# Row numbers of the first tile loaded apart, gathers without a memset between them, and finer waits in the top layers, in a recommendation tower's forward pass

## The chip, the cores and the metric

The kernel runs on one core of one Trainium2 chip. The metric is the device time of one execution in microseconds; the median of three executions before the change is 874.92 us (874.81 to 875.81).

## The reference, cut to what matters

```python
# ids (2048, 32); tbl_f (v_f, 64) with v_f 1000 to 125000; kernels (496, 64, 64); all f32
e = jnp.stack([tbl_f[ids[:, f]] for f in range(32)], axis=1)          # (2048, 32, 64)
II, JJ = np.triu_indices(32, k=1)                                     # 496 pairs
z = jnp.sum(e, axis=-1)                                               # (2048, 32)
outer = jnp.einsum('bpd,pde,bpe->bp', e[:, II], kernels, e[:, JJ])    # (2048, 496)
h = jnp.concatenate([z, outer, dense_ctx], axis=1)                    # (2048, 544)
h = jnp.maximum(h @ W_top1 + b_top1, 0.0)                             # 512 wide
h = jnp.maximum(h @ W_top2 + b_top2, 0.0)                             # 256 wide
y = h @ W_top3                                                        # (2048, 1)
```

For each sample 32 table rows are gathered, all 496 pairs of rows are multiplied through a 64 x 64 matrix of their own, and the results go through three small layers.

## The kernel before, in words

**Tiles.** The batch of 2048 is cut into six tiles of 128, 128, 256, 512, 512 and 512 samples. A "couple" k is the two tables 2k and 2k + 1; a tile has 16 couples. For each table and each 128 samples GpSimd issues one indirect DMA (L369), 512 in all, into one of eight slots of `rows`; an indirect DMA reads its row numbers from `ids_sb`, which SyncE loads whole in one transfer (L379) ahead of everything else. In the first tile GpSimd also executes a memset of a spare buffer before each gather (L368) and waits for the memset before (L367). A gather of couple n >= 8 waits until the couple eight before it has been transposed and summed.

**Steps.** When both tables of a couple have landed, TensorE transposes them (L598, `transpose_couples`) and ScalarE copies the result into `xt` (L414). VectorE sums each row for z (L535). A step (`do_step`, L615) multiplies two 64-row halves of `xt` by two 64 x 128 blocks of the pair kernels `kw`, into a PSUM bank `y`; the two halves use the upper and the lower 64 rows of the array. VectorE multiplies the result with the partner's rows (L563), and TensorE sums over the products with a strip of ones (L632, `sum_group`), into an accumulator that ScalarE copies into `h_in` (L445). The 128 steps of a tile fill four chunks of `h_in`. In narrow tiles several steps share a bank (`pack`: 4, 4, 2, 1, 1, 1). There are three `y` banks, taken in turn by all of TensorE's uses. Field sums and dense inputs are transposed (L644) into `z_in`.

**Top layers.** `mlp1` (L662, L667) is done in two pairs of 128 outputs, each with four chunks of `h_in` (128 rows) and a 64-row part of `z_in`; `mlp2` (L678) has four chunks of `h1` and two outputs halves; `mlp3` (L688) two chunks of `h2`. ScalarE applies bias and Relu (L469, L482), two activations each, and counts `act_read` up once behind the second. TensorE waits for that count (L654, L673, L684). The tables in the trace count each f32 matmul as two records.

**Order.** `PLAN` is one list by hand that all engines walk. The top layers of tile t - 1 stand in tile t, behind the first group of steps and then 8, 16 and 24 steps later (`MLP_STEPS`), each block followed by more steps; the last group of sums of tile t - 1 comes directly before the first block. For the last tile all four blocks follow its last sums at the end of the kernel. Couples 0 to 7 of the first tile are placed directly before the first step that needs them. SyncE's queue holds, in order: the row numbers, 17 chunks of `kw` (8.4 MB), biases and `w3`, `w1`, `w1z`, `w2`, and the dense inputs of each tile (L399).

Of the kernel before, what the change touches and what calls it, by code (L numbers as in the profile page):

```python
# [4 lines left out]
P = 128  # L5
# [11 lines left out]
Y_SLOTS = 3  # L17
# [110 lines left out]
PAIR_STEPS = [8, 20, 36, 56, 72, 84, 100, 116]  # L128
PAUSED_TILES = 1
MLP_STEPS = (0, 8, 16, 24)  # L130
# [77 lines left out]
def copy_use(t, k):  # L208

    for what in (("couple", t, k), ("couples", t, k), ("couples", t, k - 1)):  # L210
        if what in Y_USES:
            return Y_USES[what]
# [42 lines left out]
def tower_program(nc, dense, ids, tables, pair_k, w1, w1z, b1, w2, b2, w3, out):  # L255
# [4 lines left out]
    with ExitStack() as ctx:  # L260
# [25 lines left out]
        ident = sb("ident", [P, P])  # L286
        spare = sb("spare", [P, 2 * P])
        ones_strip = sb("ones_strip", [P, 62])

        y_banks = [bank(f"y{i}", [P, 2, TILE]) for i in range(Y_SLOTS)]  # L290
        accs = [bank(f"acc{i}", [P, TILE]) for i in range(2)]

        ids_loaded = sem("ids_loaded")
        ident_zeroed = sem("ident_zeroed")
# [7 lines left out]
        y_read = sem("y_read")  # L302
        act_read = sem("act_read")
        summed = sem("summed")
        acc_read = sem("acc_read")
        paused = sem("paused")
        fields_summed = sem("fields_summed")
# [30 lines left out]
        def _(pool):  # L338
# [5 lines left out]

            pool.wait_ge(ids_loaded, 16)
            for t in range(TILES):
                for k in range(COUPLES):
                    n = couple(t, k)
# [6 lines left out]
                    for h in range(2):  # L355
                        for c in range(rowsets(t)):
# [3 lines left out]
                            if steps > 0:  # L360

                                pool.wait_ge(y_read, steps)
                            elif t < PAUSED_TILES:
                                pauses = 2 * rowsets(t) * k + rowsets(t) * h + c
                                if pauses > 0:

                                    pool.wait_ge(paused, pauses)  # L367
                                pool.memset(spare[:], 0.0).then_inc(paused, 1)  # L368
                            pool.indirect_dma_start(  # L369
# [8 lines left out]
        def _(sp):  # L378
            sp.dma_start(ids_sb[:], ids).then_inc(ids_loaded, 16)  # L379
            first = 0  # L380
# [22 lines left out]
        def _(act):  # L403
# [50 lines left out]
            def read_mlp1(t, pair):  # L454
                u = y_use("mlp1", t, pair)
                w = WIDTHS[t]
                if t == 0 and pair == 0:

                    act.wait_ge(small_loaded, 48)
                elif pair == 0:  # L460

                    act.wait_ge(y_full, y_use("mlp2", t - 1, 0) + 1)

                    act.wait_ge(out_stored, 16 * t)

                act.wait_ge(y_full, u + 1)
                for h in range(2):
                    j = 2 * pair + h
                    last = nc.scalar.activation(h1[:, j, 0:w], y_banks[u % Y_SLOTS][:, h, 0:w], ACT.Relu,  # L469
                                                bias=b1_sb[:, j:j + 1])  # L470
                last.then_inc(act_read, 1)

            def read_mlp2(t):
# [6 lines left out]
                act.wait_ge(y_full, u + 1)  # L480
                for j in range(J2):
                    last = nc.scalar.activation(h2[:, j, 0:w], y_banks[u % Y_SLOTS][:, j, 0:w], ACT.Relu,  # L482
                                                bias=b2_sb[:, j:j + 1])
                last.then_inc(act_read, 1)

# [32 lines left out]
        def _(dve):  # L518
# [47 lines left out]
            for what, t, n in PLAN:  # L566
                if what == "couple":
                    field_sums(t, n)
                elif what == "couples":
                    field_sums(t, n)  # L570
                    field_sums(t, n + 1)
                elif what == "step" and n in runs[t]:
# [3 lines left out]
        def _(pe):  # L576
# [71 lines left out]
            def mlp1(t, pair):  # L648
                if pair == 0:
# [3 lines left out]

                    pe.wait_ge(acc_read, CHUNKS * (t + 1))  # L654

                    pe.wait_ge(act_read, act_uses_through(y_use("fields", t, 0)))
                w = WIDTHS[t]
                y = take_y(y_use("mlp1", t, pair))
                for h in range(2):
                    j = 2 * pair + h  # L660
                    for c in range(CHUNKS):
                        nc.tensor.matmul(y[:, h, 0:w], w1_sb[:, c, j * P:(j + 1) * P], h_in[:, c, 0:w],  # L662
                                         start=c == 0, stop=False)
                for h in range(2):
                    part = slice(DIM * h, DIM * h + DIM)
                    j = 2 * pair + h
                    last = nc.tensor.matmul(y[:, h, 0:w], w1z_sb[part, j * P:(j + 1) * P], z_in[part, 0:w],  # L667
                                            start=False, stop=True)
                last.then_inc(y_full, 1)

            def mlp2(t):

                pe.wait_ge(act_read, act_uses_through(y_use("mlp1", t, 1)))  # L673
                y = take_y(y_use("mlp2", t, 0))
                w = WIDTHS[t]
                for j in range(J2):
                    for c in range(J1):
                        last = nc.tensor.matmul(y[:, j, 0:w], w2_sb[:, c, j * P:(j + 1) * P], h1[:, c, 0:w],  # L678
# [3 lines left out]
            def mlp3(t):  # L682

                pe.wait_ge(act_read, act_uses_through(y_use("mlp2", t, 0)))  # L684
                y = take_y(y_use("mlp3", t, 0))
                w = WIDTHS[t]
                for c in range(J2):
                    last = nc.tensor.matmul(y[0:1, 0, 0:w], w3_sb[:, c:c + 1], h2[:, c, 0:w],  # L688
                                            start=c == 0, stop=c == J2 - 1)
# [76 lines left out]
```

## Time and profile before

| | |
|---|---|
| median of three executions | 874.92 us |
| profiled execution | 875.68 us |
| its span, first to last instruction | 873.9 us |
| TensorE (PE) busy | 840.1 us, 96% |
| VectorE (DVE) busy | 623.2 us, 71% |
| GpSimd (POOL) busy | 494.5 us, 57% |
| ScalarE (ACT) busy | 151.9 us, 17% |
| DMA | 28.32 MB |

The profiled execution is one execution; what its span leaves out (1.8 us) lies before the first and behind the last instruction. In the timelines PE is matmul and PEld the weight load; a letter q behind an engine is its queue or sequencer. "idle before" is the engine's time without work before an instruction, with what released it. A chain of waits is followed back from the last instruction: at each step to what released it.

### The profile page before, as it was taken

The page shows a single profiled execution, that of the slowest core. Times are in us where ns is not written, and L with a number is a line of the kernel's source. Part 1 is how long each engine was busy: PE and PEld are TensorE (multiplying, and loading weights), DVE is VectorE, ACT ScalarE, POOL GpSimd, SP SyncE. Part 2 cuts the span into 40 slices and gives each one's busy share as a digit, 9 for nine tenths or more (in the row PEclk, how much of TensorE's full clock was granted, in tenths as well). Part 3 has the DMA queues.
Part 4 walks back from the last instruction along what each step waited for, and adds up shares of the span by engine and source line. Part 5 has one row for each costly group of instructions (what it writes and reads, how often), then busy time and mean ns, then how long its engine had stood idle before and what let it go on. Part 6 is the DMA issues. An engine that isn't in the chain of part 4 may idle for free.

```text
span 873.9 us, 15786 instructions
## 1 busy us (share of the span) xinstructions
PE 840.1 (96%) x6584; PEld 404.9 (46%) x6584; DVE 623.2 (71%) x706; ACT 151.9 (17%) x273; POOL 494.5 (57%) x550
## 2 busy tenths in 40 slices
PE   1899999999999999999999999999999999999997
PEld 1788888766655333333333333333333333333332
DVE  0677577688866788888855488888845588888840
ACT  1212312212210220020210320020211312020001
POOL 7875777777777777777776477667723430000000
DMA  9511111111111111111111011111100000000000
GB/s 325 187 28 23 28 31 29 28 28 31 28 28 27 28 27 27 30 28 27 28 26 25 17 25 26 23 27 27 26 12 13 16 14 1 1 1 1 1 1 1
DMA packets 24209, 28.32 MB, mean 32 GB/s; under 512 B 13254, under 2 KB 13385, under 8 KB 24012
## 3 DMA queue, kind: packets, MB, share of 16 engines
q0 software_dynamic: 16384, 16.81, 10.7%
q1 hardware_dynamic: 7744, 10.49, 3.6%
q8 instruction: 54, 0.88, 0.4%
q14 instruction: 15, 0.12, 0.0%
q10 hardware_dynamic: 12, 0.01, 0.0%
HBM read 27.27 MB, written 0.01 MB: 31 GB/s over the span
## 4 chain that ended last, share of the span: by engine, by line
PE 92%; DVE 3%; POOL 2%; DMA 1%; issue 1%; ACT 1%; DVEq 0%; ACTq 0%
PE y L615 50%; PE acc L632 26%; PE y L662 7%; PE y L598 4%; PE y L678 3%; DVE prod L563 3%; POOL rows L369 2%; PE y L667 1%; DMA rows<-tbl,ids_sb 1%; PE y L688 1%; POOL spare L368 1%; DMA ids_sb<-ids 0%; ACT h_in L445 0%; PE y L644 0%; ACT h L482 0%
## 5 line engine op out<-in xcount | busy, mean ns | idle before, releaser
L563 DVE TENSOR_TENSOR prod<-y,xt 128x1024 f32<-128x1024 f32 (+2 forms) x600 | 582.4, 1033 | 199.4 <-PE y L615 198.3
L369 POOL DMA_INDIRECT rows<-tbl,ids_sb x512 | 483.4, 944 | 214.0 <-issue 111.2
L615 PE MATMUL y<-xt,kw 64*128 64x512 f32 (+2 forms) x2976 | 476.9, 463 | 4.3 <-DVE prod L563 3.2
L615 PEld LDWEIGHTS y<-xt,kw 64*128 64x128 f32 x2976 | 244.0, 190 | 217.0 <-issue 199.4
L632 PE MATMUL acc<-prod,ones_strip 128*32 128x512 f32 (+2 forms) x2976 | 239.4, 454 | 0.3 <-DVE prod L563 0.3
L632 PEld LDWEIGHTS acc<-prod,ones_strip 128*32 128x32 f32 x2976 | 79.4, 109 | 142.4 <-issue 68.1
L414 ACT COPY xt<-y 128x1024 f32<-128x1024 f32 (+3 forms) x56 | 36.2, 646 | 300.8 <-PE y L598 300.7
L662 PE MATMUL y<-h_in,w_sb 128*128 128x512 f32 (+2 forms) x192 | 58.4, 457 | 3.1 <-ACT h_in L445 2.6
L598 PE MATMUL y<-ident,rows 128*128 128x128 f32 x256 | 41.4, 289 | 20.5 <-DMA rows<-tbl,ids_sb 20.4
L535 DVE TENSOR_REDUCE z_rows<-rows 128x8 f32<-128x512 f32 (+2 forms) x96 | 44.6, 500 | 17.2 <-DMA rows<-tbl,ids_sb 17.2
L445 ACT COPY h_in<-acc 128x512 f32<-128x512 f32 (+2 forms) x24 | 10.6, 443 | 240.4 <-PE acc L632 240.4
L598 PEld LDWEIGHTS y<-ident,rows 128*128 128x128 f32 x256 | 28.0, 142 | 45.5 <-issue 33.3
L662 PEld LDWEIGHTS y<-h_in,w_sb 128*128 128x128 f32 x192 | 31.1, 190 | 31.2 <-issue 21.5
L678 PE MATMUL y<-h,w_sb 128*128 128x512 f32 (+2 forms) x96 | 28.9, 454 | 1.4 <-ACT h L469 1.4
L469 ACT ACTIVATE h<-y,b_sb 128x512 f32<-128x512 f32 (+2 forms) x24 | 11.8, 541 | 83.0 <-PE y L667 83.0
L678 PEld LDWEIGHTS y<-h,w_sb 128*128 128x128 f32 x96 | 15.6, 191 | 13.2 <-issue 10.6
L433 ACT COPY xt<-xt 64x1024 f32<-64x1024 f32 (+2 forms) x24 | 18.3, 762 | 0.6
L431 ACT COPY xt<-xt 64x1024 f32<-64x1024 f32 (+2 forms) x24 | 18.2, 758 | 0.6
L429 ACT COPY xt<-xt 64x512 f32<-64x512 f32 (+2 forms) x24 | 11.4, 474 | 15.6 <-DVE prod L563 15.4
L368 POOL MEMSET spare<- 128x256 f32 x32 | 10.5, 327 | 2.0 <-DMA ids_sb<-ids 2.0
L430 ACT COPY xt<-xt 64x512 f32<-64x512 f32 (+2 forms) x24 | 11.4, 476 | 0.6
L435 ACT COPY xt<-xt 64x512 f32<-64x512 f32 (+2 forms) x24 | 11.4, 475 | 0.6
(22 smaller groups left out, 55.1 us busy)
## 6 DMA issues: line engine op xcount, KB each, us to landing
rows<-tbl,ids_sb POOLq DMA_INDIRECT x512
kw<-pair_k SPq DMA_DIRECT2D x14, 512.0 KB, 11.9
w_sb<-w SPq DMA_DIRECT2D x1, 1024.0 KB, 12.2
w_sb<-w SPq DMA_DIRECT2D x1, 512.0 KB, 13.6
kw<-pair_k SPq DMA_DIRECT2D x1, 384.0 KB, 18.3
ids_sb<-ids SPq DMA_DIRECT2D x1, 256.0 KB, 2.7
kw<-pair_k SPq DMA_DIRECT2D x1, 256.0 KB, 4.2
w1z_sb<-w1z SPq DMA_DIRECT2D x1, 256.0 KB, 12.3
```

Of the source, the lines that this page charges most:

```text
L368: pool.memset(spare[:], 0.0).then_inc(paused, 1)
L369: pool.indirect_dma_start(out=rows[:, s, c, h, :], out_offset=None, in_=tables[f], in_offset=bass.IndirectOffsetOnAxis(ap=ids_sb[:, b, f:f ...
L414: nc.scalar.copy(xt[:, s:s + count, 0:w], y_banks[u % Y_SLOTS][:, 0:count, 0:w]).then_inc(act_read, 1)
L431: nc.scalar.copy(xt[DIM:P, x0:x3 + 1:3, 0:w], xt[DIM:P, d:d + 1, 0:w].to_broadcast([DIM, 2, w])).then_inc(extra_made, 1)
L433: nc.scalar.copy(xt[0:DIM, x1:x2 + 1, 0:w], xt[0:DIM, e:e + 1, 0:w].to_broadcast([DIM, 2, w])).then_inc(extra_made, 1)
L535: nc.vector.reduce_sum(z_rows[:, 0:rowsets(t), 0, 2 * k:2 * k + 2], rows[:, n % GATHER_SLOTS, 0:rowsets(t), :, :], axis=mybir.AxisListType ...
L563: nc.vector.tensor_tensor(prod_part(t, d, n), y_part(t, d, n), x, ALU.mult).then_inc(y_read, n)
L598: last = nc.tensor.transpose(y[:, h, P * c:P * c + P], rows[:, s, c, :, :].rearrange("p h d -> p (h d)"), ident[:])
L615: last = nc.tensor.matmul(y[:, h, :], kw[part, d, :], xt[part, slot_of(t, units[h][0] // 2), 0:w], start=True, stop=True)
L632: last = nc.tensor.matmul(acc[32 * q:32 * q + 32, 0:w], ones_strip[:, 30 - 2 * s:62 - 2 * s], prod_part(t, u // 2)[:, u % 2, :], start=s = ...
L662: nc.tensor.matmul(y[:, h, 0:w], w1_sb[:, c, j * P:(j + 1) * P], h_in[:, c, 0:w], start=c == 0, stop=False)
L678: last = nc.tensor.matmul(y[:, j, 0:w], w2_sb[:, c, j * P:(j + 1) * P], h1[:, c, 0:w], start=c == 0, stop=c == J1 - 1)
```

## The change

The row numbers come in two transfers, first those of the first tile (16 KB), then the rest (240 KB), each with a semaphore; GpSimd waits for the second at the second tile. The memset and its wait between the first tile's gathers are gone, with the spare buffer. Each Relu activation counts up a semaphore: the first of two `half_read`, the second `act_read`. `mlp1` now waits at first for three chunks of `h_in`, multiplies these and the field part for both halves, and then waits for the fourth and multiplies it for both. `mlp2` loops over chunks outside and output halves inside, and waits for each chunk; `mlp3` waits for each half of `h2`. Two rewritings in `copy_use` and the VectorE loop change no instruction.

```diff
-PAUSED_TILES = 1
...
+        first_ids_loaded = sem("first_ids_loaded")
...
+        half_read = sem("half_read")
...
-            pool.wait_ge(ids_loaded, 16)
+            pool.wait_ge(first_ids_loaded, 16)
             for t in range(TILES):
+                if t == 1:
+
+                    pool.wait_ge(ids_loaded, 16)
...
-                            elif t < PAUSED_TILES:
-                                pauses = 2 * rowsets(t) * k + rowsets(t) * h + c
-                                if pauses > 0:
-
-                                    pool.wait_ge(paused, pauses)
-                                pool.memset(spare[:], 0.0).then_inc(paused, 1)
...
-            sp.dma_start(ids_sb[:], ids).then_inc(ids_loaded, 16)
+            sp.dma_start(ids_sb[:, 0:rowsets(0), :], ids[:, 0:rowsets(0), :]).then_inc(first_ids_loaded, 16)
+            sp.dma_start(ids_sb[:, rowsets(0):, :], ids[:, rowsets(0):, :]).then_inc(ids_loaded, 16)
...
-                for h in range(2):
+                for h, done in enumerate((half_read, act_read)):
                     j = 2 * pair + h
-                    last = nc.scalar.activation(h1[:, j, 0:w], y_banks[u % Y_SLOTS][:, h, 0:w], ACT.Relu,
-                                                bias=b1_sb[:, j:j + 1])
-                last.then_inc(act_read, 1)
+                    nc.scalar.activation(h1[:, j, 0:w], y_banks[u % Y_SLOTS][:, h, 0:w], ACT.Relu,
+                                         bias=b1_sb[:, j:j + 1]).then_inc(done, 1)
...
-                for j in range(J2):
-                    last = nc.scalar.activation(h2[:, j, 0:w], y_banks[u % Y_SLOTS][:, j, 0:w], ACT.Relu,
-                                                bias=b2_sb[:, j:j + 1])
-                last.then_inc(act_read, 1)
+                for j, done in enumerate((half_read, act_read)):
+                    nc.scalar.activation(h2[:, j, 0:w], y_banks[u % Y_SLOTS][:, j, 0:w], ACT.Relu,
+                                         bias=b2_sb[:, j:j + 1]).then_inc(done, 1)
...
-                    pe.wait_ge(acc_read, CHUNKS * (t + 1))
-
                     pe.wait_ge(act_read, act_uses_through(y_use("fields", t, 0)))
+
+                    pe.wait_ge(acc_read, CHUNKS * (t + 1) - 1)
...
-                    for c in range(CHUNKS):
+                    for c in range(CHUNKS - 1):
                         nc.tensor.matmul(y[:, h, 0:w], w1_sb[:, c, j * P:(j + 1) * P], h_in[:, c, 0:w],
                                          start=c == 0, stop=False)
...
-                    last = nc.tensor.matmul(y[:, h, 0:w], w1z_sb[part, j * P:(j + 1) * P], z_in[part, 0:w],
-                                            start=False, stop=True)
+                    nc.tensor.matmul(y[:, h, 0:w], w1z_sb[part, j * P:(j + 1) * P], z_in[part, 0:w],
+                                     start=False, stop=False)
+
+                pe.wait_ge(acc_read, CHUNKS * (t + 1))
+                for h in range(2):
+                    j = 2 * pair + h
+                    last = nc.tensor.matmul(y[:, h, 0:w], w1_sb[:, CHUNKS - 1, j * P:(j + 1) * P],
+                                            h_in[:, CHUNKS - 1, 0:w], start=False, stop=True)
                 last.then_inc(y_full, 1)
 
             def mlp2(t):
-
-                pe.wait_ge(act_read, act_uses_through(y_use("mlp1", t, 1)))
-                y = take_y(y_use("mlp2", t, 0))
+                u = y_use("mlp2", t, 0)
                 w = WIDTHS[t]
-                for j in range(J2):
-                    for c in range(J1):
+                for c in range(J1):
+                    if c % 2 == 0:
+
+                        pe.wait_ge(half_read, 3 * t + c // 2 + 1)
+                    else:
+
+                        pe.wait_ge(act_read, act_uses_through(y_use("mlp1", t, c // 2)))
+                    if c == 0:
+                        y = take_y(u)
+                    for j in range(J2):
                         last = nc.tensor.matmul(y[:, j, 0:w], w2_sb[:, c, j * P:(j + 1) * P], h1[:, c, 0:w],
                                                 start=c == 0, stop=c == J1 - 1)
                 last.then_inc(y_full, 1)
 
             def mlp3(t):
 
-                pe.wait_ge(act_read, act_uses_through(y_use("mlp2", t, 0)))
+                pe.wait_ge(half_read, 3 * t + 3)
                 y = take_y(y_use("mlp3", t, 0))
                 w = WIDTHS[t]
                 for c in range(J2):
+                    if c == J2 - 1:
+
+                        pe.wait_ge(act_read, act_uses_through(y_use("mlp2", t, 0)))
```

## Rows read from the trace of the kernel before

**Rows 1.** page, part 1: engine, busy us (share of the span), instructions

```profile
PE 840.1 (96%) x6584; PEld 404.9 (46%) x6584; DVE 623.2 (71%) x706; ACT 151.9 (17%) x273; POOL 494.5 (57%) x550
```

**Rows 2.** waits of TensorE, whole span: us in total, times, longest us

```profile
PE y L598 <- DMA rows<-tbl,ids_sb: 20.4, 7, 11.9
...
PE y L662 <- ACT h_in L445: 2.6, 4, 0.7
PE y L688 <- ACT h L482: 1.4, 1, 1.4
PE y L678 <- ACT h L469: 1.4, 1, 1.4
...
PE y L662 <- issue: 0.4, 1, 0.4
```

**Rows 3.** timeline of PE, first tile: start us, us, line, shapes, count [idle before]

```profile
11.87 0.45 PE L598 MATMUL y<-ident,rows 128*128 128x128 f32 x1 [11.87 <-DMA rows<-tbl,ids_sb]
...
22.75 0.47 PE L598 MATMUL y<-ident,rows 128*128 128x128 f32 x1 [0.56 <-DMA rows<-tbl,ids_sb]
...
25.98 2.08 PE L615 MATMUL y<-xt,kw 64*128 64x128 f32 x16
28.88 0.47 PE L598 MATMUL y<-ident,rows 128*128 128x128 f32 x1 [0.82 <-DMA rows<-tbl,ids_sb]
29.29 3.79 PE L615 MATMUL y<-xt,kw 64*128 64x128 f32 x32
...
36.17 1.16 PE L615 MATMUL y<-xt,kw 64*128 64x128 f32 x16 [0.16 <-DVE prod L563]
```

**Rows 4.** chain that ended last, three pieces: start us, us, what

```profile
0.75 2.65 DMA ids_sb<-ids
...
22.82 6.02 DMA rows<-tbl,ids_sb
...
233.63 2.37 DMA rows<-tbl,ids_sb
```

**Rows 5.** busy time by stretch: engines' busy us, granted clock, DMA share, GB/s

```profile
12.00:30.00 18.00, 9.83 (x61) 7.18 (x63) 5.55 (x15) 3.85 (x13) 15.87 (x26) 1.00 1.03 386
```

**Rows 6.** timeline of SP and POOL, start of the first tile

```profile
0.75 0.38 SPq L379 DMA_DIRECT2D ids_sb<-ids  x1
...
3.92 1.10 POOL L369 DMA_INDIRECT rows<-tbl,ids_sb  x1 [0.16 <-issue]
...
5.52 0.95 POOL L369 DMA_INDIRECT rows<-tbl,ids_sb  x1 [0.17 <-issue]
...
6.96 0.95 POOL L369 DMA_INDIRECT rows<-tbl,ids_sb  x1 [0.17 <-issue]
```

**Rows 7.** timeline of POOL, start of the second tile

```profile
51.27 0.94 POOL L369 DMA_INDIRECT rows<-tbl,ids_sb  x1 [0.30 <-issue]
```

**Rows 8.** page, part 6: DMA issues, count, KB each, us to landing

```profile
kw<-pair_k SPq DMA_DIRECT2D x1, 128.0 KB, 2.5
```

**Rows 9.** chain that ended last, around two first-layer blocks in mid-kernel

```profile
90.13 0.92 PE y L615 x16
...
456.17 3.63 PE y L615 x16
...
461.65 7.06 PE y L662 x16
468.72 1.06 PE y L667 x4
469.78 3.44 PE y L615 x16
```

**Rows 10.** timeline of the weight loads (PEld) of L662

```profile
844.59 0.19 PEld L662 LDWEIGHTS y<-h_in,w_sb 128*128 128x128 f32 x1 [0.24 <-issue]
```

**Rows 11.** timeline of the tail, ACT and PE

```profile
859.99 1.26 ACT L469 ACTIVATE h<-y,b_sb 128x512 f32<-128x512 f32 x2 [6.78 <-PE y L667]
...
869.86 1.88 PE L688 MATMUL y<-h,w_sb 128*1 128x512 f32 x4 [1.42 <-ACT h L482]
```

More of the change, by code:

```diff
@@ L208, in copy_use @@
 def copy_use(t, k):
-    for what in (("couple", t, k), ("couples", t, k), ("couples", t, k - 1)):
+    for what in [("couple", t, k)] + [("couples", t, k), ("couples", t, k - 1)]:
         if what in Y_USES:
@@ L286, in tower_program @@
         ident = sb("ident", [P, P])
-        spare = sb("spare", [P, 2 * P])
         ones_strip = sb("ones_strip", [P, 62])
@@ L303, in tower_program @@
         act_read = sem("act_read")
+        half_read = sem("half_read")
         summed = sem("summed")
         acc_read = sem("acc_read")
-        paused = sem("paused")
         fields_summed = sem("fields_summed")
@@ L569, in _ @@
                 elif what == "couples":
-                    field_sums(t, n)
-                    field_sums(t, n + 1)
+                    for k in range(n, n + 2):
+                        field_sums(t, k)
                 elif what == "step" and n in runs[t]:
```

## The prediction, made before the changed kernel was run

> **What bounds the kernel now.** I began with the page's first part: TensorE is busy for 840.1 us, 96% of the span [rows 1]. So a microsecond counts only where TensorE stands still, or where its instructions get longer. The view of who waited for whom, kept to TensorE, gives all of its stops [rows 2]: 20.4 us for gathered rows, 2.6 + 0.4 us in front of the first top layer (L662), and 1.4 us each in front of the second (L678) and the third (L688). The change aims at exactly these; everything else in the 873.9 us stays.
>
> Where the 20.4 us lie the timeline tells. The seventh couple of tables (k = 6) is the last that TensorE waits for in the first tile: it is idle for 0.82 us and transposes at 28.88, and from there on the steps carry it [rows 3]. The chain of waits says who is late: one gather's data, 6.02 us from the start of its issue to landing [rows 4]. In this stretch the DMA engines are full: their share is 1.03 from 12 to 30 us, at 386 GB/s, most of it the pair kernels `kw` [rows 5]. A gather in a quiet stretch takes 2.37 us by the same view [rows 4].
>
> **Part 1, head of the kernel.** GpSimd issues the first tile's 32 gathers with a memset before each: 5.52 to 6.96 is 1.44 us per gather [rows 6]. In the second tile, where no memset stands between, one takes 0.94 us after 0.30 us of issue, 1.25 us start to start [rows 7]. So 0.19 us goes for each gather behind the first.
> The row numbers landed at 0.75 + 2.65 = 3.40 us [rows 4], and the first gather started at 3.92 [rows 6]. Without the memset it needs some 0.3 us of issue [rows 7], so 0.2 us is won. The transfer shrinks from 256 KB to 16 KB. No row has this size; the nearest is 128 KB of `kw` in 2.5 us [rows 8] against 2.65 for the 256 KB [rows 4]. That would give 0.15 us, and the same slope carried on to 16 KB 0.3; I take 0.2. The ends are 0 (all is latency) and 0.6 us. The second transfer of row numbers puts one more issue on SyncE ahead of all of `kw`, 0.38 us by the first one's row [rows 6]. Nothing feels that: a chunk of `kw` of 128 KB lands after 2.5 us [rows 8], and TensorE has no rows to work on before 11.87 [rows 3]. The new wait at the second tile is for a transfer that has been in for 40 us by then.
> Couple 6 ends with the 14th gather: 0.2 + 0.2 + 13 x 0.19 = 2.9 us earlier. If the time to landing stays at 6.02 us, its rows are there at 28.84 - 2.9 = 25.9. Can TensorE take them? Couple 4 (10th gather) comes 2.1 us earlier, at 20.6 instead of 22.75. From there to the end of couple 5's steps TensorE needs at today's rates 28.06 - 22.75 = 5.3 us [rows 3], which ends at 25.9. So both arrive together and all 2.9 us are won, with next to no slack. What is late next: couple 7 was wanted at 33.0, after the 3.79 us of couple 6's steps, and comes by the same count by 28.4, wanted then at 30.1; couple 8 comes by 31.0 and is wanted behind one more group, at about 30.1 + 1.6 = 31.7 (an estimate between 16 records' 1.16 and 2.08 us). The second of these covers by 0.7 us only. Later gathers have the eight slots as their bound, not the pace.
> Ends for this part: 0, if landings do not follow the issue, and 4.6 us, if TensorE's rate changes too (rival 2).
>
> **Part 2, the first top layer in tiles 0 to 4.** The wait for the fourth chunk now stands behind three chunks and the field sums. At 512 wide a full block of 16 matmul records takes 7.06 us [rows 9], so twelve take 5.3, far more than the copy of the last chunk. The stops in front of L662 (3.0 us, [rows 2]) go: four put down to the copy, with the longest at 0.7 us, which I take to be the tail's, and one of 0.4. That leaves 2.3 us in mid-kernel.
> But the order of kinds changes. After a full-height block the steps' 16 records of 64 rows take 3.63 us, directly after the field matmuls (64 rows as well) 3.44 [rows 9]: 0.19 us for the change from full height to half. The four field records show it too: 1.06 us, where a quarter of 3.44 is 0.86. The other direction is seen in the full block: the weight loads come every 0.19 + 0.24 = 0.43 us [rows 10], 16 x 0.43 = 6.88, and it takes 7.06: again 0.18. At 128 wide the steps behind the field matmuls take 0.92 us in the chain [rows 9], against 1.16 behind a stop [rows 3], so a narrow tile pays as well. Today the order is sum, full, field, step: two changes of height per pair. It becomes sum, full, field, full, step: four. Ten pairs of the five tiles lie between steps, where TensorE has no slack: 10 x 2 x 0.19 = 3.8 us lost. Ends: 1.9 (if only the change to half height costs) and 4.0. So the middle loses 3.8 - 2.3 = 1.5 us.
> The Trainium skill (TensorEngine Tiling (Array Packing), the numbered limits of tiling) says that changing the tiling mode drains the engine. It gives no time; the trace agrees, with 0.19 us.
>
> **Part 3, the tail.** Behind the last step nothing covers anything. In front of L662: 0.7 us go. In front of L678: 1.4 us go, for chunks 0 and 1 come from the pair read long before; their four matmuls take 4 x 0.88 = 3.5 us, and the first of the two activations [rows 11] ends after 0.63. In front of L688: two activations, 1.26 us as in the layer before, become one, 0.63 [rows 11]; the second is hidden behind the first matmul, half of 1.88 us. 0.6 us go. Changes of height: sum, full, field, full, field, full both before and after (the new last block of pair 0 runs on into pair 1), so no loss. Tail: 2.7 us. The mlp2 order (chunks outside, halves inside) changes no count and no shape; the new increments ride on activations. I cost them at nothing.
>
> **Sum.** 2.9 (head) - 1.5 (middle) + 2.7 (tail) = 4.1 us. The profiled execution took 875.68 us, 0.8 over the median, with a span of 873.9; it would become 871.6 and the span 869.8. Against the median of 874.92 the forecast is 870.8 us. A measurement here can tell about 0.2% (1.75 us) from no change.
>
> **Rivals.**
> Rival 1: the landings do not follow. With the engines at a share of 1.03 a gather is served between the large packets of `kw`; if the queue's share of them sets the pace, earlier issues only wait longer. For it: 6.02 against 2.37 us to landing [rows 4]. Against: a queue that falls behind would show a growing time to landing, and it does not grow: the second gather, issued from 5.52 [rows 6], lets TensorE start at 11.87 [rows 3], 6.35 us later, the fourteenth after 6.02. The head gives 0 and the time is 873.7: no change by the bound.
> The Trainium skill (DMA: Bandwidth & Descriptors, section on SWDGE, HWDGE and iDMA) says that the engine goes round-robin between the queues of the two kinds; by that a gather waits its turn but is not crowded out, and the sum would be mine.
> Rival 2: TensorE's rate rises sooner. The granted clock stands at 1.00 (2.4 GHz) from 12 to 30 us [rows 5], but the step records say otherwise: 16 of them take 2.08 us at 25.98 and 1.16 at 36.17, and the 32 at 29.29 still 3.79 [rows 3]: the rate of the lower level, 1.2 GHz, up to 33.0. In front of that rise TensorE had stopped twice for gathers (0.56, 0.82). With gathers earlier those stops shrink and work comes closer together; if couple 6's 32 records run fast, 3.79 becomes some 2.1: 1.7 us more, 869.1.
> Rival 3: the rise stays at 33.0 whatever TensorE does. Then the work between 30.1 and 33.0 is at the slow rate, two groups at 0.92 us extra each: the head gives 1.1 and the time is 872.6.
> Rival 4, slower than before: the denser but thinner stream puts the rise off further. From 30.1 us on, slow work costs 0.79 of its fast time (2.08 / 1.16). To end over 876.7 it must eat 4.1 + 1.8 = 5.9 us: 7.5 us of fast work, done in 13.4, so the low rate would last to 43.5 us instead of 33. It decides from there on. Against: TensorE has fewer stops than before; for: the column does not show the level, so I can't see what moves it.
> The skill (TensorE: Matmul & The Clock Gate, the part on the clock gate) warns that trn2's clock events in a trace can be unreliable; rows 3 against rows 5 bear it out.
>
> **How the numbers follow.** Forecast 0.47; rival 1 0.15; rival 2 0.15; rival 3 0.17; rival 4 0.06. Rivals 1 and 3 give the slow side, rival 3 straddles the 0.2% bound (873.2) with a quarter of its chance. Faster 0.47 + 0.15 + 0.13 = 0.75, same 0.15 + 0.04 = 0.19, slower 0.06. Range: rival 2 with the large end of the row numbers' transfer and 0.5 us for small errors, 868.4; above rival 1 with 0.2 us, 873.9. Rival 4 and what spills over the ends is left out.
>
> **What would show it.** Gathers start every 1.25 us from 3.5; couple 6's transpose is at 26.0 and the first fast steps 3 us earlier. No stop in front of L662 and L678, 0.6 to 0.8 left in front of L688. In the middle every first-layer pair is 0.38 us longer, split by the field matmuls. The time from the end of the last sum to the end is 2.7 us shorter. I am wrong in the head if the transpose of couple 6 is later than 27, in the middle if blocks of four full matmuls behind the fields run without a gap, in the tail if a stop over 0.2 us is left in front of L678.

## The result, and the profile after

Four executions of each kernel, alternating on one chip: 868.95 us median after (868.28 to 869.07) against 875.37 before. The ratio is 0.9925, 95% interval 0.9908 to 0.9942, so 6.4 us are gone where 4.1 were forecast; 868.95 lies inside the range of 868.4 to 873.9, near its lower end. The profiled span went from 873.9 to 867.2 us, by 6.7, and it is this pair of executions that is taken apart below. One execution of each can carry up to 1.3 us that are not the change's: of 23 executions of the kernel before, in the experiments' first group, nine took 874.05 to 874.62 us and fourteen 875.35 to 876.47, and the one taken apart here, at 875.68, belongs with the upper ones. What parts the two is not shown, since the one trace of this kernel is of the upper kind.

The page of the changed kernel, parts 1 and 2 in part:

```profile
span 867.2 us, 15755 instructions
PE 842.1 (97%) x6584; PEld 403.7 (47%) x6584; DVE 622.6 (72%) x706; ACT 151.9 (18%) x273; POOL 483.9 (56%) x518
```

TensorE is busy for 2.0 us more than before [rows 1], in a span 6.7 us shorter. So 8.7 us of its stops went, and 2.0 of that were paid back in work. Its waits, by the same view as [rows 2]:

```profile
PE y L593 <- DMA rows<-tbl,ids_sb: 16.1, 4, 10.9
PE y L610 <- DVE prod L558: 3.5, 9, 0.7
PE y L698 <- ACT h L478: 0.8, 1, 0.8
```

The wait for gathered rows fell from 20.4 us in seven places to 16.1 in four. The waits of the first and second top layer (now L657 and L685) are gone from the list, and the third (L698) keeps 0.8 of 1.4.

To see where the time went I put marks into both timelines and compared their times. The kernel before, TensorE, at its first group of sums, at the gather wait that follows 230 us, and at its last group of sums:

```profile
37.27 1.95 PE L632 MATMUL acc<-prod,ones_strip 128*32 128x128 f32 x64
...
236.05 0.65 PE L598 MATMUL y<-ident,rows 128*128 128x128 f32 x4 [0.71 <-DMA rows<-tbl,ids_sb]
...
841.00 1.92 PE L632 MATMUL acc<-prod,ones_strip 128*32 128x512 f32 x16 [0.29 <-DVE prod L563]
```

The changed kernel at the same three places:

```profile
33.04 1.96 PE L627 MATMUL acc<-prod,ones_strip 128*32 128x128 f32 x64
...
231.67 1.09 PE L593 MATMUL y<-ident,rows 128*128 128x128 f32 x8
...
837.13 1.92 PE L627 MATMUL acc<-prod,ones_strip 128*32 128x512 f32 x16 [0.29 <-DVE prod L558]
```

The head is 4.2 us shorter (37.27 to 33.04), at the last sums the lead (how much earlier the changed kernel is at the same place) is 3.9 (841.00 to 837.13), at the end 6.7. So the **head gives 4.2** (forecast 2.9), the **middle costs 0.4** (forecast 1.5) and the **tail gives 2.8** (forecast 2.7). The eight transposes at 231.67 run through, where four of them waited 0.71 us before.

The head of the changed kernel, GpSimd and TensorE:

```profile
2.68 1.10 POOL L365 DMA_INDIRECT rows<-tbl,ids_sb  x1 [1.21 <-DMA ids_sb<-ids]
4.08 0.94 POOL L365 DMA_INDIRECT rows<-tbl,ids_sb  x1 [0.30 <-issue]
5.33 0.94 POOL L365 DMA_INDIRECT rows<-tbl,ids_sb  x1 [0.30 <-issue]
```

```profile
17.51 0.48 PE L593 MATMUL y<-ident,rows 128*128 128x128 f32 x1 [2.00 <-DMA rows<-tbl,ids_sb]
17.92 2.08 PE L610 MATMUL y<-xt,kw 64*128 64x128 f32 x16
...
25.18 0.47 PE L593 MATMUL y<-ident,rows 128*128 128x128 f32 x1
25.58 2.94 PE L610 MATMUL y<-xt,kw 64*128 64x128 f32 x32
28.45 0.33 PE L593 MATMUL y<-ident,rows 128*128 128x128 f32 x1
29.25 1.16 PE L610 MATMUL y<-xt,kw 64*128 64x128 f32 x16 [0.47 <-DVE prod L558]
```

The gathers start 1.25 us apart, the first at 2.68 instead of 3.92 [rows 6]. Couple 6 is transposed at 25.18 instead of 28.88 [rows 3], without a wait. Its 32 step records take 2.94 us instead of 3.79, which is the slow rate for somewhat under half of them and the fast one for the rest. From couple 3 on TensorE waits for no gather; what couple 3 waits for is its second gather, by the chain:

```profile
11.57 5.90 DMA rows<-tbl,ids_sb
```

In mid-kernel the chain shows what the new order costs (tile 3's second pair, beside [rows 9]):

```profile
457.48 5.35 PE y L657 x12
462.82 1.06 PE y L662 x4
463.88 1.91 PE y L668 x4
465.80 3.63 PE y L610 x16
```

Full, field, full, step: 11.95 us. Before it was 7.06 + 1.06 + 3.44 = 11.56 [rows 9]. Four full records took a quarter of 6.88, or 1.72, and now take 1.91; the steps take 3.63 again. Both changes of height (the height is the number of array rows that a matmul uses, 128 or 64) cost 0.19 us, as reckoned. The tail, by the chain:

```profile
855.49 6.88 PE y L685 x16
...
862.46 0.70 ACT h L478
...
863.20 1.89 PE y L698 x4
```

The second layer starts the moment the first ends, at 853.58 + 1.91 in the chain, and a single activation stands in front of the third.

### The profile page after: what moved, and what is told of

Its sections match the earlier page's. It is cut to its first block, busy times and chain, and to the rows that moved or that the text cites. A ratio compares the mean times of both kernels' runs of the same rounds, so it can differ in the third digit from the quotient of the medians.

```text
span 867.2 us, 15755 instructions
## 1 busy us (share of the span) xinstructions
PE 842.1 (97%) x6584; PEld 403.7 (47%) x6584; DVE 622.6 (72%) x706; ACT 151.9 (18%) x273; POOL 483.9 (56%) x518
## 4 chain that ended last, share of the span: by engine, by line
PE 95%; DVE 2%; DMA 1%; issue 1%; POOL 1%; ACT 0%; DVEq 0%; ACTq 0%
PE y L610 52%; PE acc L627 26%; PE y L657 5%; PE y L593 4%; PE y L685 3%; DVE prod L558 2%; PE y L668 2%; PE y L662 1%; PE y L698 1%; POOL rows L365 1%; DMA rows<-tbl,ids_sb 1%; PE y L639 0%; DMA ids_sb<-ids 0%; DVEq L259 0%; ACT h L478 0%
## 5 line engine op out<-in xcount | busy, mean ns | idle before, releaser
L593 PE MATMUL y<-ident,rows 128*128 128x128 f32 x256 | 41.2, 288 | 16.2 <-DMA rows<-tbl,ids_sb 16.1
L657 PE MATMUL y<-h_in,w_sb 128*128 128x512 f32 (+2 forms) x144 | 44.4, 458 | 0.1
L657 PEld LDWEIGHTS y<-h_in,w_sb 128*128 128x128 f32 x144 | 23.3, 190 | 21.6 <-issue 18.0
L685 PE MATMUL y<-h,w_sb 128*128 128x512 f32 (+2 forms) x96 | 28.8, 453 | 0.0
L685 PEld LDWEIGHTS y<-h,w_sb 128*128 128x128 f32 x96 | 15.6, 191 | 11.5 <-issue 10.7
L668 PE MATMUL y<-h_in,w_sb 128*128 128x512 f32 (+2 forms) x48 | 17.0, 477 | 0.0
L426 ACT COPY xt<-xt 64x512 f32<-64x512 f32 (+2 forms) x24 | 11.4, 474 | 15.6 <-DVE prod L558 15.4
L427 ACT COPY xt<-xt 64x512 f32<-64x512 f32 (+2 forms) x24 | 11.4, 476 | 0.6
```

Source lines behind the costliest of these rows:

```text
L593: last = nc.tensor.transpose(y[:, h, P * c:P * c + P], rows[:, s, c, :, :].rearrange("p h d -> p (h d)"), ident[:])
L668: last = nc.tensor.matmul(y[:, h, 0:w], w1_sb[:, CHUNKS - 1, j * P:(j + 1) * P], h_in[:, CHUNKS - 1, 0:w], start=False, stop=True)
```

## The experiments

**Row numbers alone.** The kernel before, with this edit only (and a wait for `ids_loaded` at the second tile):

```diff
-            pool.wait_ge(ids_loaded, 16)
+            pool.wait_ge(first_ids_loaded, 16)
...
-            sp.dma_start(ids_sb[:], ids).then_inc(ids_loaded, 16)
+            sp.dma_start(ids_sb[:, 0:rowsets(0), :], ids[:, 0:rowsets(0), :]).then_inc(first_ids_loaded, 16)
+            sp.dma_start(ids_sb[:, rowsets(0):, :], ids[:, rowsets(0):, :]).then_inc(ids_loaded, 16)
```

> The kernel before with the row numbers in two transfers and nothing else. Theory (each part's price adds up): the first transfer lands 1.66 us after its issue as in the changed kernel, not 2.65, so every gather of the first tile is 1.0 us earlier and the span 1.0 us shorter. Rival (the head is worth something only because TensorE's rate rises sooner, which needs the closer gathers): under 0.3 us.

Measured: ratio 0.9995 (0.9986 to 1.0004), span 873.6 against 873.9. The first part of the theory held: the chain has 1.74 us for the 16 KB. The second fell. TensorE's timeline says why:

```profile
27.81 0.33 PE L602 MATMUL y<-ident,rows 128*128 128x128 f32 x1 [0.81 <-DMA rows<-tbl,ids_sb]
28.08 2.06 PE L619 MATMUL y<-xt,kw 64*128 64x128 f32 x32
30.62 0.33 PE L602 MATMUL y<-ident,rows 128*128 128x128 f32 x1 [0.48 <-DMA rows<-tbl,ids_sb]
30.88 1.36 PE L619 MATMUL y<-xt,kw 64*128 64x128 f32 x16
33.09 0.33 PE L602 MATMUL y<-ident,rows 128*128 128x128 f32 x1 [0.85 <-DMA rows<-tbl,ids_sb]
33.35 3.53 PE L619 MATMUL y<-xt,kw 64*128 64x128 f32 x32
```

Couple 6 is 1.07 us earlier and its records already run fast, but then couples 7 and 8 are waited for, since the gathers still come 1.44 us apart. The cover that couples 7 and 8 had before was TensorE's own slowness. One edit moved the wait two couples down. And the rate fell back behind those stops: the next row of 32 records reads 3.53 us (at 33.35), and the granted clock 0.87 from 30 to 35 us. The fall is not in every execution: the mean clock was 0.998 in five of eleven, this one among them, which took 875.21 to 875.55 us, and 1.000 in the six others, with 873.27 to 874.70. Those six are no lower than the lower nine of the kernel before.

**Memsets alone.**

```diff
-PAUSED_TILES = 1
+PAUSED_TILES = 0
```

> The kernel before with only the memsets between the gathers left out. Theory: gathers 1.25 us apart, couple 6 is 2.7 us earlier, and the step records turn fast sooner by at least as much; 3.0 to 3.5 us off the span. Rival (landings follow the share of the DMA queues, not the issue): the time from issue to landing grows past 6.5 us and under 1.5 us is won.

Measured: ratio 0.9972 (0.9961 to 0.9984), medians 872.09 against 875.37, span 870.3, 3.6 us less. Couple 6 is transposed at 26.07, 2.8 us earlier; the tenth gather takes 5.70 us to landing in the chain. The 3.6 us hold an accident, though. These executions part in two as well, and this trace is one of the lower five (871.7 to 872.21), which lie 2.3 us under the lower nine of the kernel before; the upper two (873.0 and 873.05) lie 2.6 us under the upper fourteen. Both are close to the count of 2.7. So the memsets were most of the head, and the closer gathers do not land slower. In the full change the first sums begin at 33.04, here at 33.66: on top of it the row numbers are worth 0.6 us, by one trace of each.

**Top layers alone.** The changed kernel with the whole transfer and the memsets put back.

> The changed kernel's top layers alone, with the old row numbers' transfer and the memsets. Theory: the tail gives 2.8 us; the middle loses 20 changes of height at 0.19 us and wins the stops in front of the first layer, but the loss up to 236 us is taken up by the gather that TensorE waited 0.7 us for there: 2.2 us off the span. Rival (changes of height cost nothing, the middle is a gain): 4.5 us or more.

Measured: ratio 0.9971 (0.9962 to 0.9980), medians 872.9 against 875.37, span 871.4: 2.5 us less, where 2.2 were expected (lower beside lower it is 2.2, upper beside upper 2.4). The wait at the gather after 230 us is not there (eight transposes run through at 235.86). The three parts alone give 0.3 + 3.6 + 2.5 = 6.4 us of span, together they gave 6.7; by the means of all executions it is 0.3 + 2.9 + 2.5 = 5.7 against 6.6. With executions that scatter by over a microsecond this does not settle whether the parts simply add up.

**Field matmuls last.** The changed kernel; the wait for the fourth chunk stays where it was, but the field matmuls stand behind it again, next to the steps, which are of their height.

```diff
-                for h in range(2):
-                    part = slice(DIM * h, DIM * h + DIM)
-                    j = 2 * pair + h
-                    nc.tensor.matmul(y[:, h, 0:w], w1z_sb[part, j * P:(j + 1) * P], z_in[part, 0:w],
-                                     start=False, stop=False)
-
                 pe.wait_ge(acc_read, CHUNKS * (t + 1))
                 for h in range(2):
                     j = 2 * pair + h
-                    last = nc.tensor.matmul(y[:, h, 0:w], w1_sb[:, CHUNKS - 1, j * P:(j + 1) * P],
-                                            h_in[:, CHUNKS - 1, 0:w], start=False, stop=True)
+                    nc.tensor.matmul(y[:, h, 0:w], w1_sb[:, CHUNKS - 1, j * P:(j + 1) * P],
+                                     h_in[:, CHUNKS - 1, 0:w], start=False, stop=False)
+                for h in range(2):
+                    part = slice(DIM * h, DIM * h + DIM)
+                    j = 2 * pair + h
+                    last = nc.tensor.matmul(y[:, h, 0:w], w1z_sb[part, j * P:(j + 1) * P], z_in[part, 0:w],
+                                            start=False, stop=True)
```

> The changed kernel with the field matmuls put back behind the fourth chunk (its wait stays just before the fourth chunk). Theory: two changes of height of 0.19 us go in each of ten pairs, 3.8 us of TensorE; but GpSimd issues gathers without a pause from 70 to 230 us, so the wait for a gather at the turn from the third to the fourth tile comes back and eats 0.9 to 1.3 of it: 2.5 to 2.9 us less than the changed kernel, and the wait is in the trace. Rival (no such bound): 3.8 us less. Rival (the gap is not from the height): no difference.

Measured: 866.29 us median, ratio to the kernel before 0.9903 (0.9888 to 0.9918), span 864.5: 2.7 us less than the changed kernel, by medians as by spans. And the wait is back, longer than it ever was:

```profile
229.60 0.66 PE L593 MATMUL y<-ident,rows 128*128 128x128 f32 x4
231.52 0.66 PE L593 MATMUL y<-ident,rows 128*128 128x128 f32 x4 [1.27 <-DMA rows<-tbl,ids_sb]
```

3.8 us of changes of height went and 1.27 came back as this wait. The lead over the changed kernel bears out the price: it grows by 1.7 us over the four pairs before the wait and by 2.2 over the six behind it, 0.4 a pair. Another 0.3 us of the 2.7 are the execution's: they lie in the head, where nothing was edited, since the rate rose sooner in couple 6's records (2.94 us in the changed kernel):

```profile
25.64 2.55 PE L610 MATMUL y<-xt,kw 64*128 64x128 f32 x32
```

Why the wait stands where it does GpSimd's timeline of the changed kernel tells:

```profile
70.84 0.94 POOL L365 DMA_INDIRECT rows<-tbl,ids_sb  x1 [5.04 <-PE y L593]
```

It stops for 5.04 us, until a slot is free, and from there on issues a gather nearly every 1.25 us up to this place. TensorE can be up to a point later there for nothing: this is where part of the new order's cost went.

**Held-back chunks and early matmuls.** Two edits to the changed kernel, alone and together with the field matmuls last. SyncE holds the later chunks of `kw` until the steps come near; TensorE transposes the identity in its idle time ahead of the first seven couples, 31 times in all. The added matmuls compute nothing that is used.

```diff
+KW_FREE, KW_LEAD = 5, 40
...
             for c, n in enumerate(K_CHUNKS):
+                if c >= KW_FREE:
+                    sp.wait_ge(y_read, max(1, first - KW_LEAD))
                 sp.dma_start(kw[:, first:first + n, :],
```

```diff
+FILLERS = [16, 3, 3, 3, 2, 2, 2]
...
                 if what == "couple":
+                    for _ in range(FILLERS[n] if t == 0 and n < len(FILLERS) else 0):
+                        nc.tensor.transpose(accs[1][:, 0:P], ident[:], ident[:])
                     transpose_couples(t, n, 1)
```

Chunks held:

> The changed kernel with the pair kernels' chunks from the sixth on held back until the steps have come within 40 steps of them, so that the DMA engines are not full while the first gathers land. Theory (a gather's 5.9 us to landing are 2.4 us plus queueing behind that load): couples 2 to 8 land after 2.4 to 3.5 us, the first steps start 2.5 to 3.5 us earlier, and 2.5 to 3.5 us are won in all. Rival (the time to landing comes from the gathers themselves, issued so closely): still over 5 us to landing, nothing won, or a loss where a held chunk is late.

Transposes on the changed kernel:

> The changed kernel with 31 transposes of the identity in TensorE's idle time ahead of the first seven couples (into the accumulator that is not yet in use). Theory (TensorE's rate rises with its own work): step records take 1.2 us for 16 from the first group on instead of 2.08; couple 6 can then not be earlier than its gather, so the couples' landings set the pace, waits for gathers come back in front of couples 4 to 8, and 0.3 to 1.0 us is won. Rival (the rise stands at a fixed time near 28 to 33 us, whatever TensorE does): the first three groups still take 2.08 us and nothing is won.

Both, with the field matmuls last:

> The changed kernel with the field matmuls last, the held-back chunks and the 31 transposes. Theory: against the kernel with the field matmuls last alone 3.0 to 4.0 us less, with the couples' gathers now setting the pace of the whole first tile's start. Rival (the gather that TensorE waits for at 231 us moves with GpSimd's unbroken issue and not with the head): under 1 us less, and that wait grows by what the head won.

Transposes on the kernel before:

> The kernel before with the same 31 transposes. Theory: the rate is up from the first group of steps, so the work behind couple 6 is 1.7 us shorter, but couples 7 and 8 then have to be waited for (as with the row numbers in two transfers), so the span is 0.3 to 1.0 us shorter and no more. Rival (rate at a fixed time): no change, and the 32 records behind couple 6 still take 3.79 us.

These four ran beside a kernel before that took 1166.6 us. The ratios to it were 0.9948 (0.9928 to 0.9968) for the held chunks, 0.9968 (0.9944 to 0.9992) for the transposes, 0.9928 (0.9901 to 0.9956) for both, and 1.0003 (0.9984 to 1.0023) for the transposes on the kernel before. TensorE's waits in the last of these show what kind of execution it is:

```profile
PE acc L633 <- issue: 51.4, 78, 1.6
PE y L616 <- DVE prod L564: 44.8, 25, 7.7
PE y L616 <- issue: 41.7, 25, 7.9
```

"issue" is time in which nothing that the profile shows was waited for; it strikes the narrow tiles, which have the most instructions per microsecond. In the head itself TensorE stands 5 to 18 us in front of single groups of steps, so what the edits are worth there cannot be read from these runs. One thing can, as it comes before those stops: with the transposes alone the first 16 step records still took 2.08 us, in the changed kernel (at 18.24) as in the kernel before (at 20.51). The two kernels that mattered most were run again, with the kernel before at 875 us.

> The same kernel as the first one with held-back chunks (the changed kernel otherwise), again, since the kernel before took 1166 us beside that one, with TensorE stopped for lack of instructions. Theory (5.9 us to landing are 2.4 us plus queueing behind the pair kernels' load): couples 2 to 8 land after 2.4 to 3.5 us, the first steps start 2.5 to 3.5 us earlier, and 2.5 to 3.5 us less than the changed kernel in all. Rival (the time to landing is the closely issued gathers' own): over 5 us to landing, nothing won.

Measured: 866.82 us median, ratio 0.9897 (0.9882 to 0.9912) with the kernel before at 875.26. Couple 3's second gather, and TensorE:

```profile
11.61 0.94 POOL L366 DMA_INDIRECT rows<-tbl,ids_sb  x1 [0.30 <-issue]
```

```profile
14.08 0.48 PE L596 MATMUL y<-ident,rows 128*128 128x128 f32 x1 [1.52 <-DMA rows<-tbl,ids_sb]
...
23.04 0.33 PE L596 MATMUL y<-ident,rows 128*128 128x128 f32 x1 [1.26 <-DMA rows<-tbl,ids_sb]
23.30 2.06 PE L613 MATMUL y<-xt,kw 64*128 64x128 f32 x32
...
29.87 1.96 PE L630 MATMUL acc<-prod,ones_strip 128*32 128x128 f32 x64
...
64.65 0.30 PE L642 MATMUL y<-ident,z_rows 128*128 128x128 f32 x1 [1.62 <-issue]
```

Couple 3 is transposed at 14.08 instead of 17.51. Its second gather is issued at 11.61, so it landed in under 2.5 us, where the same gather, issued at 11.57 in the changed kernel, took 5.90. The DMA share between 8 and 20 us is 0.35 here; in the kernel before it is 1.03, as in the changed one. So the long time to landing is the load beside it, not the gathers' spacing. At the first sums the head has 3.2 us more (33.04 to 29.87). At the end it is 2.2 by the spans and 2.1 by the medians, where 2.5 to 3.5 were expected: 1.62 go in front of the field transpose L642, of which 0.69 come back, as the changed kernel's wait for VectorE behind that transpose falls away (the steps start at 64.88 instead of 67.15). Beside the field sums that transpose needs the dense inputs, which SyncE now issues only from 55.19 on, behind the held chunks; that they are what it waits for is argued from the order of the queue, the row does not name them. The wait at 231 us does not come back: the eight transposes run through at 229.45. GpSimd's unbroken issue starts earlier as well, since it is TensorE that frees the slot it starts with:

```profile
68.56 0.94 POOL L366 DMA_INDIRECT rows<-tbl,ids_sb  x1 [5.94 <-PE y L596]
```

> The same kernel as the one with field matmuls last, held-back chunks and 31 transposes, again for the same reason. Theory: 3.0 to 4.0 us less than the kernel with the field matmuls last alone, so about 862.5 us where the kernel before takes 875; the steps' rate is up before the first group (1.2 us for 16 records, not 2.08) and the couples' gathers set the pace up to couple 8. Rival (TensorE waits at 230 us for a gather that moves with GpSimd's unbroken issue and not with the head): under 1 us less, and that wait grows by what the head won.

Measured: 866.62 us median, ratio 0.9887 (0.9871 to 0.9904). That cannot be told from the field matmuls last alone (0.9903), though one of its five executions took 863.66 and the others 866.07 to 866.70. The theory fell, and TensorE's timeline shows two reasons in a row:

```profile
14.42 1.25 PE L614 MATMUL y<-xt,kw 64*128 64x128 f32 x16
...
21.68 0.48 PE L597 MATMUL y<-ident,rows 128*128 128x128 f32 x1 [2.93 <-DMA rows<-tbl,ids_sb]
22.09 2.08 PE L614 MATMUL y<-xt,kw 64*128 64x128 f32 x16
...
24.93 3.63 PE L614 MATMUL y<-xt,kw 64*128 64x128 f32 x32
...
231.87 0.65 PE L597 MATMUL y<-ident,rows 128*128 128x128 f32 x4 [1.60 <-DMA rows<-tbl,ids_sb]
```

The rate was up before the first group, as meant: the first group takes 1.25 us at 14.42, where the changed kernel's takes 2.08 at 17.92. But the first finished steps released several held chunks at once, and the gather of couple 5 met them: 5.05 us from issue to landing in the chain (from 16.59). TensorE stood for 2.93 us and went on at the slow rate up to 28.5. What was won in front was lost again: the first sums begin at 32.76, with the field matmuls last alone at 32.71. So the rival, that the wait at 231 us eats what the head wins, was not put to the test; that wait is 1.60 us here and 1.27 there.

Two further kernels had the field matmuls last, chunks released one at a time (`KW_LEAD` 24) and the first dense inputs ahead of them, without and with the transposes. The kernel before took 1154.99 us beside them.

> Field matmuls last; the pair kernels' chunks from the sixth on held until the steps are within 24 of them, so that one is released at a time and no burst meets a gather; the first tile's dense inputs sent ahead of the held chunks, so that the field transpose no longer waits for them. Theory: couple 6 is transposed at 22.3 instead of 23.0, no wait at the field transpose (1.6 us in the first kernel with held chunks), and all of the head's 3.2 to 4.0 us reach the end: 862 to 863 us where the kernel before takes 875.3. Rival (GpSimd's unbroken issue of gathers up to 230 us is what ends last): 865 to 866, with the wait there at 2 us or more.

> The kernel beside it with the 31 transposes of the identity in TensorE's idle time. Theory (the 2.93 us stop of the earlier kernel with transposes came from the burst of held chunks, not from the transposes): the fast rate holds from the first group on, couples 4 to 8 are each waited for, as GpSimd issues a couple in 2.5 us, and 0.5 to 1.5 us less than the kernel beside it. Rival (TensorE falls back to the slow rate in those stops): within 0.5 us of it, either way.

Measured: ratios 0.9940 (0.9919 to 0.9962) and 0.9935 (0.9913 to 0.9956), with TensorE stopped for 53 us in all by "issue" in front of its sums. The head of the second shows that the transposes do not raise the rate every time. Up to the first steps its transposes lie within 0.2 us of those of the kernel at 866.62 us, and still the first group is slow:

```profile
14.57 2.08 PE L618 MATMUL y<-xt,kw 64*128 64x128 f32 x16
```

No wait at the field transpose is among the longest in either. What the two kernels give beside a kernel before at 875 us is open. The best times measured beside that are the field matmuls last (866.29), and the two kernels with held chunks (866.82 and 866.62), which are alike within their intervals.

## Why the prediction was right, point by point

**What bounds it** held: time went only where TensorE stopped or its work grew.

**Head, the mechanism right, the size short.** The sum had 2.9 us, the mark shows 4.2, beside one of the upper executions of the kernel before. How much of the 1.3 between them comes from that is open; it may be nearly all. Three terms, by the two traces:
- The spacing was right, 1.25 us. Memsets alone moved couple 6 by 2.8 us; my count without the transfer's 0.2 was 2.7.
- The transfer of the row numbers was mis-sized: I took 0.2 us, with 0.6 as the far end, from a row of 128 KB. It landed in 1.66 us against 2.65 [rows 4], so 1.0 us. With it the first gather was 1.24 us earlier, not 0.4. Alone, this is worth almost nothing; next to the memsets, 0.6 us.
- I held TensorE's rate to rise with the steps. It rose sooner, in the middle of couple 6's records (2.94 us for 3.79): rival 2, in half. With the transfer, this is the missing 1.3 us, part of which a wait of 0.47 us for VectorE takes back. Where in the records the rise falls is partly luck: with this same head it was 2.55 us in another execution.

**"Landings stay at 6.02 us"** held: 5.90 in the changed kernel. Rival 1 fell with it, and the chunks held back show its cause, the queue behind `kw`, with under 2.5 us for the same gather. By the round-robin between the queues (the Trainium skill, DMA: Bandwidth & Descriptors, the section on SWDGE, HWDGE and iDMA) a gather waits its turn; the runs agree that it is not crowded out, and that the turn costs 3.4 us.

**Rivals 3 and 4** fell. The fast rate began near 33 us with the old gathers (kernel before, top layers alone), near 27 to 28 with the new (and with the row numbers alone), near 22 with chunks held, and before 15 in both traces of the kernel with chunks held, transposes and the field matmuls last. After a stop of 2.93 us the slow rate was back. That is no fixed time. It goes with TensorE's own work, but what of that work decides is open: the same transposes left the first group at 2.08 us in three other traces. The granted clock, by the view of busy time by stretch, reads 1.00 (2.4 GHz) in the kernel before and the changed one all through the first 50 us, though 16 records took 2.08 us early and 1.16 later. Yet it does show a fall once the fast rate has been reached, in the run with the field matmuls last, held chunks and transposes at 866.62 us (us; PE busy, PEld, DVE, ACT, POOL; granted clock, DMA share, GB/s):

```profile
15.00:20.00 5.00, 2.89 (x33) 1.98 (x31) 2.77 (x5) 2.26 (x7) 3.78 (x5) 1.00 0.57 170
20.00:25.00 5.00, 3.32 (x22) 2.55 (x22) 1.07 (x4) 0.27 (x1) 3.78 (x5) 0.65 0.57 200
25.00:30.00 5.00, 5.00 (x50) 4.56 (x49) 3.49 (x9) 0.53 (x2) 3.78 (x5) 0.67 0.33 66
```

1.00, then 0.65 and 0.67, a mixture of the two levels, where the records are slow again; from 22 to 24 us alone it reads 0.50 (1.2 GHz). In these executions the column is right after the first rise and says nothing of the slow start. The Trainium skill's warning (TensorE: Matmul & The Clock Gate, the part on the clock gate) that such events can be unreliable fits the start alone.

**Middle, the term that failed.** "The middle loses 3.8 - 2.3 = 1.5 us" left out that TensorE waited for a gather at 236 us, in [rows 2] as part of 20.4 us, and that GpSimd's stream does not care how fast TensorE is there. The price of a change of height held, 0.19 us twice per pair. (At 128 wide I set 0.92 us from the chain against 1.16 from the timeline; by the chain alone those 16 records went from 0.92 to 1.11, again 0.19.) The stops went as forecast. But TensorE gained 0.9 us at 231 because its wait ended (0.71) and its eight transposes ran together. The lead tells it by stretches: from 4.2 at the first sums it falls to 3.0 just before that place, where four pairs less one stop make 1.1; it is 3.95 right behind it; and 3.9 at the last sums, where six pairs less three stops of 0.5, 0.7 and 0.7 should have taken 0.4. These last 0.3 us were not taken apart. The experiment with the field matmuls last shows both: 3.8 us fewer changes of height, 1.27 us of wait in return, 2.7 us in the end, 0.3 of them the execution's.

**Tail:** 2.8 us for 2.7, with each stop as predicted: none, none, 0.84 us.

**Covers named:** "couple 8 covers by 0.7 us" held, with no wait for it. In the experiment with the row numbers alone the same two couples were the new wait, which the prediction did not look at, since the two edits came together.

**Range:** its low end is 0.2 us off as added up. Rival 2's 869.1, less 0.4 for the row numbers' large end and 0.5 for small errors, is 868.2, not 868.4; 868.95 is inside both. That 6.4 us came where 4.1 were forecast is two things: a middle that cost 1.1 less, 0.9 of it by the wait left out, and a head up to 1.3 larger, depending on the execution that it is compared with.

## What to carry to other kernels

When a wait is refined by splitting a block of matmuls, look at which heights of the array end up side by side: an order that returns to half height costs 0.19 us each way in a place where the engine has no slack, and putting the odd piece next to its like took 2.7 us off this kernel with the same wait hidden. Before adding up parts, find the one engine that runs without a break (here GpSimd's gathers, one every 1.25 us from 71 to 230 us): between the start and the end of that stretch costs of others may be free, and gains may be eaten, while what moves its start is passed on. And before spacing small transfers differently, see what large load they land beside.

## What the runs showed of the hardware that was not expected

- 16 KB of row numbers landed in 1.66 us (1.74 in the kernel with that edit alone), 256 KB in 2.65 and 240 KB in 2.7: a first small piece comes a full microsecond earlier at the start, if something can use it.
- The same kernel before took 875 us in three of the groups of runs and 1155 to 1167 us in two others, with TensorE stopped by "issue" in the 128-wide tiles. In those executions its granted clock was 0.89 to 0.92 on average. What starves it there was not tried.
